# All nine tap products of the deformable convolution on VectorE from the third tile on, and the slot table behind the last tile

## What is computed

```
x = x + dcn(group_norm(x))           # 3x3 deformable convolution, 9 taps, offsets and masks computed from the input
t = t + mamba_both_ways(layer_norm(t))   # two selective scans, forward and backward
t = t + moe(layer_norm(t), edge_index)   # graph attention over 262144 edges makes the gate, top 2 of 4 experts
```

```
s[k, y, x] = wy[k, y] * wx[k, x]        # the tap product; the mask is already in wx
out = sum over k of s[k] @ (x @ kernel[k])
```

## Time and profile before

| | |
|---|---|
| median of 3 runs | 646.47 us (646.43 to 647.82) |
| the profiled execution | 647.57 us, its span 645.8 us |
| DVE busy | 535.7 us, 83% of the span |
| PE busy | 468.8 us, 73% |
| POOL busy | 344.8 us, 53% |
| ACT busy | 242.6 us, 38% |
| mean granted clock of PE | 0.83 of full speed |

### The profile page before, as it was taken

One profiled execution on the slowest core, in us unless ns is written; L12 is line 12 of the kernel. 1 busy time (PEld: TensorE's weight loads), 2 busy tenths in 40 slices (PEclk: granted clock), 3 DMA queues, 4 the chain that ended last, 5 costly groups with the idle time before them and its releaser, 6 DMA issues.

```text
span 645.8 us, 6879 instructions
## 1 busy us (share of the span) xinstructions
PE 468.8 (73%) x2535; PEld 291.7 (45%) x2535; DVE 535.7 (83%) x836; ACT 242.6 (38%) x297; POOL 344.8 (53%) x197
## 2 busy tenths in 40 slices
PE   2896989987993998977777876598787888722200
PEld 2255878876982894422222322244433454512200
DVE  4999996997499343388989999999999977787897
ACT  1442413515132136778434344434444405621120
POOL 5153161456063000144699899979989817777303
PEclk9796578987797699988688899989999996855555
DMA  6410000000000001130365775546655401111100
GB/s 195 112 38 1 1 1 3 2 10 1 1 1 8 2 9 46 57 106 33 131 191 172 219 212 211 174 159 244 207 191 183 148 10 10 9 8 8 5 1 32
DMA packets 29587, 50.85 MB, mean 79 GB/s; under 512 B 16144, under 2 KB 18480, under 8 KB 29232
## 3 DMA queue, kind: packets, MB, share of 16 engines
q1 hardware_dynamic: 27760, 49.82, 24.3%
q0 software_dynamic: 1792, 0.58, 1.7%
HBM read 48.62 MB, written 1.77 MB: 78 GB/s over the span
## 4 chain that ended last, share of the span: by engine, by line
DVE 49%; PE 23%; POOL 14%; issue 6%; ACT 6%; DMA 2%; DVEq 0%; SPq 0%; POOLq 0%; ACTq 0%
DVE arena L1582 15%; POOL arena L605 9%; PE ps L676 7%; DVE ps L1572 6%; POOL arena L559 4%; PE ps L845 3%; DVE arena L1358 3%; PE ps L698 3%; DVE arena L1373 2%; PE ps L724 2%; DVE arena L1404 1%; PE ps L661 1%; PE ps L782 1%; POOL arena L552 1%; DVE arena L1356 1%
## 5 line engine op out<-in xcount | busy, mean ns | idle before, releaser
L1582 DVE TENSOR_TENSOR_SCAN arena<-arena,ps 128x1024 f32<-128x1024 f32 x64 | 144.8, 2280 | 10.2 <-POOL arena L559 2.8
L845 PE MATMUL ps<-arena,ident 128*128 128x512 f32 x256 | 130.2, 633 | 20.9 <-POOL arena L559 20.9
L534 POOL TENSOR_TENSOR arena<-arena 128x1536 f32<-128x1536 f32 (+2 forms) x16 | 65.6, 4106 | 111.0 <-DVE arena L1262 60.0
L559 POOL TENSOR_TENSOR arena<-arena 128x1024 f32<-128x1024 f32 x48 | 112.4, 2353 | 23.0 <-PE ps L845 11.9
L1110 ACT ACTIVATE arena<-arena,neg_a 128x1020 f32<-128x1020 f32 x64 | 73.1, 1145 | 120.2 <-DVE arena L1582 116.1
L676 PE MATMUL ps<-arena 128*128 128x64 f32 x576 | 81.0, 311 | 12.5 <-DVE x_tok L1290 12.5
L676 PEld LDWEIGHTS ps<-arena 128*128 128x128 f32 x576 | 80.2, 227 | 12.9 <-issue 12.9
L845 PEld LDWEIGHTS ps<-arena,ident 128*128 128x128 f32 x256 | 49.8, 201 | 71.3 <-issue 36.8
L605 POOL DMA_INDIRECT arena<-node_rows,src_idx x56 | 56.1, 1003 | 31.2 <-issue 16.8
L1572 DVE TENSOR_TENSOR ps<-arena,ps 128x1024 f32<-128x1024 f32 x48 | 58.0, 1208 | 0.3 <-PE ps L835 0.2
L1017 ACT ACTIVATE arena<-ps 128x768 f32<-128x768 f32 x48 | 37.2, 808 | 48.5 <-PE ps L724 48.5
(11 more groups left out here) (344 smaller groups left out, 744.2 us busy)
## 6 DMA issues: line engine op xcount, KB each, us to landing
arena<-state_rows SPq DMA_DIRECT2D x64, 512.0 KB, 4.3
cs<-state_rows SPq DMA_DIRECT2D x16, 512.0 KB, 4.3
arena<-dram_edges SPq DMA_DIRECT2D x2, 1024.0 KB, 8.7
arena<-dram_x SPq DMA_DIRECT2D x2, 512.0 KB, 5.0
arena<-node_rows,src_idx POOLq DMA_INDIRECT x56, 2.9
x_tok<-dram_x SPq DMA_DIRECT2D x1, 512.0 KB, 11.0
res_scratch<-x_tok SPq DMA_DIRECT2D x4, 128.0 KB, 2.0
arena<-res_scratch SPq DMA_DIRECT2D x1, 512.0 KB, 3.3
```

What stands on the lines that cost most here:

```text
L534: g.tensor_tensor(s_buf[i % 2][:, kk], wy[:, i, kk].unsqueeze(3).to_broadcast([P, nk, HEIGHT, WIDTH]), wx[:, i, kk].unsqueeze(2).to_broadc ...
L559: g.tensor_tensor(gg[n % 2], hh[n % 2], cs[n % GROUP], ALU.mult).then_inc(s["g_ready"], 1)
L845: m = pe.matmul(ps[:, 4 + q, :], ident[:], gg[n % 2][:, 512 * q:512 * q + 512], start=False, stop=True, skip_group_check=True)
L1582: v.tensor_tensor_scan(o, x0, x1, 0.0, ALU.mult, ALU.add).then_inc(s["scan_ready"], 1)
```

## The change

From tile 2 on DVE makes all nine tap products, one instruction of 2304 elements instead of 768. POOL keeps its share of tiles 0 and 1, then makes the four tap weights and the two diagonals at once and has nothing more until the scans, apart from four memsets that DVE did: the edges of `xnt`, behind the slot table. `payload` moves on DVE from tile 13 to behind `taps(15)` and `conv_sum(11)`, ahead of `ln_end(1)` and `ln_first(2)`. The slot table moves on PE behind the last tile's `conv_tail(15)`, and `slot_list` on DVE behind `left_rounds`. The streams behind the table go from 26 to 6. The folded weights `wg_t` take other words of the arena, since the payload now lives longer, and PE waits for `ell_read` before the transposes of `resb`.

```diff
-DVE_TAPS = [5, 4] + [3] * (NT - 2)
+DVE_TAPS = [5, 4] + [K2] * (NT - 2)
...
-XK_STREAM, LN_STREAM, COPY_STREAM, Z_STREAM, STATS_STREAM = (24, 20), 26, 10, 12, 14
+XK_STREAM, LN_STREAM, COPY_STREAM, Z_STREAM, STATS_STREAM = (24, 20), 6, 10, 12, 14
...
-        wg_t = xs[0][0:HE, 0:2 * C]
+        wg_t = cw_b[0].rearrange("p k c -> p (k c)")[0:HE, 0:2 * C]
...
-            for i in range(NT):
-                if i % TPQ == 0:
-                    g.wait_ge(s["wx_ready"], i // TPQ + 1)
-                if i >= 2:
-                    g.wait_ge(s["st_psum"], 3 * i - 3)
+            g.wait_ge(s["wx_ready"], 1)
+            for i in range(2):
                 kk, nk = slice(DVE_TAPS[i], K2), K2 - DVE_TAPS[i]
...
+            for d in range(2):
+                tap_weights(d)
...
+            g.wait_ge(s["ell_psum"], 1)
+            for r in range(2):
+                rr = slice(C * r, C * r + C)
+                k(g.memset(xnt[rr, :, 0:TAPS - 1 - r], 0.0))
+                m = g.memset(xnt[rr, :, TAPS - 1 - r + SEQ:SEQP], 0.0)
...
-                pe.wait_ge(s["s2_ready"], i + 1)
+                if i < 2:
+                    pe.wait_ge(s["s2_ready"], i + 1)
...
-                elif i == TABLE_AT:
-                    slot_table()
             conv_tail(NT - 1)
             pe.wait_ge(s["left_count"], 1)
-            pe.wait_ge(s["ell_read"], 1)
+            slot_table()
...
                         pe.wait_ge(s["left_known"], 1)
+                        pe.wait_ge(s["ell_read"], 1)
...
-            act.wait_ge(s["da_zero"], 1)
+            act.wait_ge(s["xnt_zero"], 1)
...
                     ln_second(1)
-                    payload()
                 elif i == 14:
                     left_over()
                 elif i == 15:
+                    payload()
                     ln_end(1)
                     ln_first(2)
...
             conv_sum(NT - 3)
-            slot_list()
...
             left_rounds()
+            slot_list()
```

More of the change, by code:

```diff
@@ L40 @@
 WCH = len(W_AT) - 1
-COUNT_AT, BASE_AT, TABLE_AT = (4, 7), 9, 13
+COUNT_AT, BASE_AT = (4, 7), 9
 HATS_AT = (2, 5, 8)
@@ L354, in program @@
             own_ready base_psum base_read pay_ready ell_psum idx_ready left_psum left_count left_known
-            ell_read look_read rows_kept rows_out c_in0 c_in1 c_in2 c_in3 bx_in b_psum b_made bx_ready bx_put da_ready scan_ready last_ready g_ready g_used da_zero yg_ready
+            ell_read look_read rows_kept rows_out c_in0 c_in1 c_in2 c_in3 bx_in b_psum b_made bx_ready bx_put da_ready scan_ready last_ready g_ready g_used xnt_zero da_zero yg_ready
             fold_in fold_const fold_psum fold_ready rest_t_psum rest_t_ready b2_ready t2_psum stats2 t2_ready v_ready vt_psum vt_ready h_psum h_ready tab_out last_in nb_in0 nb_in1 nb_in2 nb_in3 e_in exp_ready
@@ L535, in _ @@
                                 wx[:, i, kk].unsqueeze(2).to_broadcast([P, nk, HEIGHT, WIDTH]), ALU.mult).then_inc(s["s2_ready"], 1)
[L536 to L546, removed]
+            g.wait_ge(s["const_ready"], 1)
+            g.wait_ge(s["cw_in"], 96)
+            for d in range(2):
+                tap_weights(d)
+            g.wait_ge(s["wmamba_in"], WMAMBA)
+            for d in range(2):
+                g.tensor_tensor(diag_d[d][:], ident[:], vec[d][:, 2:3].to_broadcast([P, P]), ALU.mult).then_inc(s["diag_ready"], 1)
+                g.wait_ge(s["diag_ready"], d + 1)
             def own_b(grp):
@@ L559, in with_c @@
                 g.tensor_tensor(gg[n % 2], hh[n % 2], cs[n % GROUP], ALU.mult).then_inc(s["g_ready"], 1)
+            g.wait_ge(s["ell_psum"], 1)
[3 more added lines that the diff above has]
+                m = g.memset(xnt[rr, :, TAPS - 1 - r + SEQ:SEQP], 0.0)
+                if r:
+                    m.then_inc(s["xnt_zero"], 1)
+                else:
+                    k(m)
             for d in range(2):
@@ L1023, in _ @@
                     act.wait_ge(s["fold_psum"], 2)
+                    act.wait_ge(s["taps_ready"], 4)
                     f(wg_t, ps[0:HE, 7, 0:2 * C], ACT.Copy).then_inc(s["fold_ready"], 1)
@@ L1042, in _ @@
             act.wait_ge(s["s_ready"], NT)
-            act.wait_ge(s["s2_ready"], NT)
             for part in range(2):
@@ L1107, in _ @@
                     act.wait_ge(s["dt_ready"], d + 1)
-                    act.wait_ge(s["da_zero"], 2 + d)
+                    act.wait_ge(s["da_zero"], 1 + d)
                 act.wait_ge(s["scan_ready"], n + 1)
```

## The result

The changed kernel takes 641.91 us (median of 16 runs) beside 646.58 us for the kernel before: the ratio is 0.9934, 95% interval 0.9911 to 0.9957, some 4.3 us less. The forecast was 637.0, that is 9.5 less. The profiled execution took 641.93 us. One run of the sixteen took 1074.64 us; it stands far apart from all the others, nothing on record says why, and the ratio leaves it out.

What follows compares the result with a forecast made beforehand. DVE and PE, neither full, wait for each other, and PE's waits bring slow tails. Terms -1.2 + 0 - 8.3 = -9.5 from 647.57 give 638.1, less 1.1 for the median: 637.0; range 628.5 to 643.5, forecast's own 632 to 643.1.

Steps and rivals of the forecast that it cites:

- All behind it follows at the same distance: Everything behind DVE's last `conv_sum` (242.3 us), scans and experts included, shifts by as much as that does.
- Behind it: After the last `conv_sum`: fewer streams, slot table, memsets on POOL, later `slot_list` and the `ell_read` wait together cost zero.
- A, to the second histogram: First stretch of the convolution, to the release of the second histogram at 134.08: 1.2 us earlier.
- The relief of the fold: POOL's products leaving DVE's fold of the keys give back 5.3 us; tile 2 was taken to start 0.4 earlier.
- The gap in front of tail 2: PE waits 2.0 us for `conv_sum(0)`, a new gap, and tail 2 runs at half clock.
- the branch in which tail 3 is slow too: In stretch A, clock low through tile 4's transposes and tail 3: A becomes +3.6 us.
- B, to the base sums: Stretch to the base sums at 172.49: three longer products (+4.8) hide under DVE's 8.68 us wait for PE; change 0.
- C, to the last `conv_sum`: Stretch to the end of tail 15: -18.4 + 1.8 + 7.6 + 0.7 = -8.3 us.
- My clock argument: A PE wait is paid twice, once itself and once as the slow tail after it: 7.91 instead of 4.13 us.
- The clock was not kept at the second gap: Case of PE keeping 2.4 GHz at the end gap only: -17.8 us, 628.7; one gap kept, either one, had chance 0.22.
- DVE was not saturated: Rival 2: DVE is saturated, the excess is not POOL's and stays; sum +0.2, 646.7, no change; chance 0.05.
- the tails of tiles 9 to 13 kept 2.4 GHz: Against rival 3: clock lost within tiles 11 to 13, 656.8 us, chance 0.08; 7.9 us tails would refute the forecast.

Runs made afterwards that it cites:

- experiment 4: The changed kernel once more, no edit: 642.46 us beside 647.98 for the kernel before, ratio 0.9928.
- Experiment 2: Changed kernel with DVE's payload behind `conv_sum(13)`, ahead of `conv_sum(14)`: 631.27 us beside 648.64 for the kernel before, ratio 0.9755.
- experiment 7: Changed kernel with payload late and `conv_sum(0)` early: 626.00 us; with exponentials first too: 622.33; with added stream matmuls as well: 621.17.
- experiment 3: Each half alone against the kernel before: nine-tap products 647.93 us, ratio 0.9976; payload, slot table, slot list and streams moved 642.45 us, ratio 0.9905.

## Why the prediction was wrong

The direction was right, the size was not, and the step that failed is one sentence: "All behind it follows at the same distance" (and the "Zero" of the part "Behind it"). The lead was 10.2 us at the end of the convolution, 0.7 more than forecast, and 5.6 at the end of the span: 1.1 went in the scans, and in the experts ACT's first exponential came 8.7 late, behind hidden layers that PE worked through at 1.2 GHz. The 641.91 lies in the forecast's own range, 632 to 643.1, by luck: the upper end of that range was a convolution that gains less, not a loss behind it.

- **A, to the second histogram:** forecast -1.2, measured -3.35 (134.08 to 130.73). The relief of the fold was undersized. PE reached tail 1 2.0 us earlier (63.51 beside 65.53), where I had tile 2 0.4 earlier. Therefore `conv_sum(0)` came at 79.5, not 81.2. The gap in front of tail 2 was there, 1.03 instead of 2.0, and so was the slow tail, but not for the reason given: I had the clock come back before this gap and fall by it, and it had not come back. That the forecast 7.91 was met is luck. In the profile of experiment 4 it went as I had said, the clock fell behind the gap, and there the branch in which tail 3 is slow too came true: +2.65 (136.73), priced at +3.6.
- **B, to the base sums:** forecast 0, measured +1.3. Not the products: x @ kernel took 1.33 instead of 0.75 and the owner sums 5.60 instead of 4.88, at a clock that was at 0.50 from 152.5 to 169.6. Before, it was at 0.50 from 157.2 to 170.9, and from 150.4 to 153.8, where the slow transposes lay in front of a wait for ACT and cost nothing.
- **C, to the last `conv_sum`:** forecast -8.3, measured -8.2. The wait before the last transposes was 2.74 where I had 1.8; the last two tails 15.62 beside 8.25 were +7.4 where I had +7.6. Experiment 2 shows that the gap makes them slow. That the sum fits to 0.1 is partly luck: the wait was 0.9 longer than forecast, and x @ kernel behind tail 12, which I had left out, took 0.75 instead of 1.33.
- **Behind it:** forecast 0. At the first state rows the lead was still 10.2. In the scans it fell to 9.1 (by the stretches under experiment 7 this goes with the nine taps on DVE, and is not explained), in the first gather pass to 0.35, and in the next three it rose to 5.6.

My clock argument was right for the end of the convolution and stopped there: I took the part behind as rigid because it held no instruction that the change touches. It held a place where the clock could come back or stay down, an ACT order in which the exponential stands behind PE's slow layers, and a DVE that had 0.32 us to spare there. All three stood in the trace of before: PE at 0.50 until 542.5, ACT's list, the wait of 0.32.

Of the rivals none happened. The clock was not kept at the second gap, and at the first there was nothing to keep in this profile; DVE was not saturated; the tails of tiles 9 to 13 kept 2.4 GHz. That POOL's silence frees DVE was right in each row, and by experiment 3 it was worth little at the end: the other half, payload, slot table, slot list and streams together, brought the gain. For the first rival I had taken the gap of 0.56 us at 179.70 as one that leaves the clock alone. Gaps of the same length do not all do so: in the kernel before the clock fell at 150.4 behind the gap of 0.56 in front of 149.97, and after the change at 97.9 behind the one in front of 97.44.

The Trainium skill (Perfetto Trace Analysis, Optimizing Scalar/DVE Operations) warns that a split between DVE and GPSIMD may not help because of their shared port. This trace agrees as far as DVE's durations go: 3.58 for three taps beside POOL, 2.56 for nine without it.

## What to carry to other kernels

A stretch that is shifted as a whole is not worth its shift until one has looked behind it for places where a wait is small on one side and the clock of PE is at its lower level on the other. A gap on PE is priced with the slow matmuls that follow it: removing 2.74 us of waiting gave 10 us. And where two engines share a list (here ACT's exponential behind Gelu copies that hang on PE), the short step that somebody waits for belongs first.

## What the hardware showed beyond that

PE's busy time alone does not bring its clock back. From 530.9 to 556.0 us after the change PE was busy for 25.08 of 25.10 us and the granted clock stayed at 0.50; from 216 to 231 us it was busy without a gap at 0.50, in the last two tails, while tail 13 had 1.00 with the same matmuls. The Trainium skill (TensorE: Matmul & The Clock Gate, Part 1: The HAM clock gate) says that the clock follows how busy PE has lately been. The trace does not agree, if busy is what the profile counts.

Why the first layers of the experts brought the clock back in the two profiles of the kernel before (exponentials as they were, and first), and in none of the nine others without added streams, stays open; the work on PE is the same, and from the stream of 14 matmuls to the second of these layers the gaps in it are too, to a few hundredths of a microsecond. One thing differs: the clock had fallen 6.0 and 6.2 us after the start of the stream of 14 matmuls in the two in which it came back, and 6.9 to 8.0 us after it in the nine (read from stretches of a quarter of a microsecond). Whether that is chance or follows from the order ahead of it was not tried.
